# The reciprocal of the softmax denominators moves from the middle to the end of VectorE's step

## The chip, the cores and the metric

The kernel runs on one core of a Trainium2 chip. The metric is the device time of one execution in microseconds (us); a kernel's time is the median of several runs. The engines are called PE (TensorE; PEld is its weight load), DVE (VectorE), ACT (ScalarE), POOL (GpSimd) and SP (SyncE).

## The reference

128 sequences of 64 tokens with 128 features pass through one layer: cross-attention with 16 heads of 8 features, and a feed-forward network of which each token uses one of 8 experts. Cut to what matters:

```python
def xattn(Q, K, V, Wq, bq, Wk, bk, Wv, bv, Wo, bo):     # 16 heads of 8
    q = split_heads(Q @ Wq.T + bq); k = split_heads(K @ Wk.T + bk); v = split_heads(V @ Wv.T + bv)
    scores = einsum('bhqd,bhkd->bhqk', q, k) / sqrt(8)
    probs = softmax(scores, axis=-1)
    out = einsum('bhqk,bhkd->bhqd', probs, v)
    return merge_heads(out) @ Wo.T + bo

def ffn(x, Wr, br, W1, b1, W2, b2):                      # 8 experts, 128 -> 512 -> 128
    expert = argmax(x @ Wr.T + br)
    y_e = relu(x @ W1[e].T + b1[e]) @ W2[e].T + b2[e]
    return y_e of each token's own expert

x = x + xattn(layernorm(x), ctx, ctx, ...)
x = x + ffn(layernorm(x), ...)
```

## The kernel before

The 8192 tokens are 64 tiles of 128 (two sequences a tile). The program is written by hand, engine by engine: each engine has its own list of instructions, runs it in order, and waits on semaphores that the others raise. There are four stretches: projections (to some 70 us), attention (to some 340 us), the end of the routing, and the expert network (from some 380 us).

In the attention stretch every engine goes through the same loop of steps, and step n of each engine works on several tiles at once, at different stages of their way. On PE, step n holds in this order: the scores of tile n (L809); the first half of the transposes of tile n-2's exponentials (L796); the product that spreads the reciprocals over the heads' features (L833, tile n-8); the output projection (L837, tile n-9); small work for the routing (L844, L851, L853, L862); the second half of the transposes (L796); numerators (L879) and denominators (L888) of tile n-3. On DVE, step n holds: the maximum over each head's scores of tile n (L627) and their subtraction (L635); `OT`, the numerators times the spread reciprocals, of tile n-8 (L651); the addition of the projected output to `X` for tile n-9 (L654); bn_stats of tile n-10 (L664), and at some steps the moments (L525 to L533, where n mod 8 is 1), the seed of an inverse root (L674 to L680, where n mod 8 is 2) or routing work for a batch of eight tiles. The scores of tile n and n+1 lie in different PSUM banks, so that PE can be one tile ahead of DVE.

The denominators of four tiles are a group: they are added up in one half of PSUM bank 5, and one reciprocal turns the whole group into `RD` (128x128). Group g is tiles 4g to 4g+3. DVE takes its reciprocal in step 4g+7. PE's step 4g+7 holds, as its last part, the denominators of tile 4g+4, the first of group g+1. They go to the other half of the same bank, and PE waits ahead of them for the reciprocals of all groups up to g:

```python
g, t = divmod(m, GT)              # m = n - 3, GT = 4
if t == 0:
    need(pe, rd_done, g)          # L884
at = P * (g % 2)
for z in range(2):
    for c in range(4):
        last = nc.tensor.matmul(bank(5)[32 * c:32 * c + 32, at:at + P], ones[:, t, z, :], ...)
last.then_inc(od_done, 1)
```

PE's next instruction is the first of the scores of step n+1. PE also waits for a group's reciprocal ahead of the first L833 of that group, in step 4g+8. DVE waits ahead of the reciprocal for the denominators of tile 4g+3, which are the end of PE's step 4g+6. POOL spreads the values of each tile into `VP` (L410) after the denominators of an earlier tile, and at the end of a batch sends eight tiles' rows to HBM (L425).

Of the kernel before, what the change touches and what calls it, by code (L numbers as in the profile page):

```python
# [14 lines left out]
P = 128  # L15
# [5 lines left out]
GT = 4  # L21
NG = NT // GT
# [58 lines left out]
L_RD = 7  # L81
# [40 lines left out]
def need(eng, sem, value):  # L122

    if not isinstance(value, int) or value > 0:
        eng.wait_ge(sem, value)
# [25 lines left out]
def build(nc, x, ctxT, wts, we, w2, con, pad, ids, out):  # L151
# [6 lines left out]
    with ctx:  # L158
        def sb(name, *shape, dt=f32):
            return ctx.enter_context(nc.sbuf_tensor(name, list(shape), dt))  # L160

        def sem(name):
            return ctx.enter_context(nc.semaphore(name))
# [47 lines left out]
        RD = sb("RD", P, 2, P)  # L211
# [36 lines left out]
        def bank(k, n=1):  # L248
            return PS[:, 512 * k:512 * (k + n)]
# [13 lines left out]
        pt_done, pt_ready, od_done, rd_done, ot_ready = (sem(n) for n in ("pt_done", "pt_ready", "od_done", "rd_done", "ot_ready"))  # L263
# [255 lines left out]
        def _(dve):  # L519
            def moments(n, st, ms, mean, var, half, gap, mv, var_read):  # L520


                m0, m1, v0, v1 = (st[:, :, k] for k in (1, 4, 2, 5))
                need(dve, mv, n)
                nc.vector.tensor_tensor(ms[:, 0, :], m0, m1, ALU.add)  # L525
                nc.vector.tensor_tensor(ms[:, 1, :], v0, v1, ALU.add)
                nc.vector.tensor_tensor(ms[:, 2, :], m0, m1, ALU.subtract).then_inc(half, 1)
                dve.wait_ge(half, n + 1)
                need(dve, *var_read)
                nc.vector.tensor_scalar(mean, ms[:, 0, :], 0.5, None, ALU.mult)  # L530
                nc.vector.scalar_tensor_tensor(ms[:, 3, :], ms[:, 2, :], 0.25, ms[:, 2, :], ALU.mult, ALU.mult).then_inc(gap, 1)
                dve.wait_ge(gap, n + 1)
                nc.vector.scalar_tensor_tensor(var, ms[:, 1, :], 1.0 / D, ms[:, 3, :], ALU.mult, ALU.add).then_inc(mv, 1)  # L533
# [87 lines left out]
            def stage2(s):  # L621
                n = s.n
                stage3_early(s)
                sc = bank(2 * (n % 2), 2).rearrange("p (h k) -> p h k", h=H)
                if n < NT:
                    dve.wait_ge(s_done, n + 1)
                    nc.vector.tensor_reduce(MX[:, n % 2, :], sc, axis=AX.X, op=ALU.max).then_inc(mx_done, 1)  # L627
                g, late = divmod(n - L_RD, GT)
                if late == 0 and 0 <= g < NG:
                    dve.wait_ge(od_done, GT * g + GT)  # L630
                    nc.vector.reciprocal(RD[:, g % 2, :], bank(5)[:, P * (g % 2):P * (g % 2) + P]).then_inc(rd_done, 1)
                if n < NT:
                    dve.wait_ge(mx_done, n + 1)
                    need(dve, pt_done, 2 * (n - 2))
                    nc.vector.tensor_tensor(SB[:, n % 3].rearrange("p (h k) -> p h k", h=H), sc,  # L635
                                            MX[:, n % 2, :].unsqueeze(2).to_broadcast([P, H, SEQ]), ALU.subtract).then_inc(sub_done, 1)


                need(dve, rdx_done, min(n - L_MUL + 1, NT))
                need(dve, wo_done, min(n - L_X1 + 1, NT))  # L640
                for i in range(4):
                    j = s.batch(M_LG + 2 * i)
                    if j is not None:
                        dve.wait_ge(lgp_done, 4 * j + i + 1)
                j = s.batch(M_RANK)
                if j is not None:
                    dve.wait_ge(rank_done, j + 1)
                m = n - L_MUL
                if 0 <= m < NT:
                    dve.wait_ge(num_kept, m + 1)  # L650
                    nc.vector.tensor_tensor(OT[:, m % 2, :], bank(7)[:, 0:P], NUM[:, m % 8, :], ALU.mult).then_inc(ot_ready, 1)  # L651
                m = n - L_X1
                if 0 <= m < NT:
                    nc.vector.tensor_tensor(X[:, m, 0:D], bank(7)[:, P:2 * P], X[:, m, 0:D], ALU.add).then_inc(x1_done, 1)  # L654
                stage3_late(s)

            def stage3_late(s):
                for t in range(ST):
                    j = s.batch(M_BN + t)
                    if j is not None:  # L660
                        if isinstance(s.n, int):
                            dve.wait_ge(x1_done, j * ST + t + 1)
                        x1 = X[:, bass.ds(j * ST + t, 1), 0:D].rearrange("p a d -> p (a d)")
                        nc.vector.bn_stats(STAT2[:, t, :], x1).then_inc(stat2, 1)  # L664
                j = s.batch(M_MOM)
                if j is not None:
                    dve.wait_ge(stat2, ST * j + ST)
                    moments(j, STAT2, MS2, X[:, bass.ds(j * ST, ST), MU], VAR2[:], half2, gap2, mv2, (inv_step, INV_STEPS * j))
                j = s.batch(M_SEED)
                if j is not None:  # L670


                    dve.wait_ge(mv2, j + 1)
                    nc.vector.tensor_scalar(VAR2[:], VAR2[:], EPS, None, ALU.add).then_inc(seed_step, 1)  # L674
                    dve.wait_ge(seed_step, 4 * j + 1)
                    nc.vector.tensor_scalar(YY[:].bitcast(i32), VAR2[:].bitcast(i32), 1, None, ALU.logical_shift_right).then_inc(seed_step, 1)
                    dve.wait_ge(seed_step, 4 * j + 2)
                    nc.vector.tensor_scalar(Y[:].bitcast(i32), YY[:].bitcast(i32), -1.0, float(0x5f3759df), ALU.mult, ALU.add).then_inc(seed_step, 1)
                    dve.wait_ge(seed_step, 4 * j + 3)
                    nc.vector.tensor_scalar(HALF[:], VAR2[:], 0.5, None, ALU.mult).then_inc(seed_step, 1)  # L680
                    dve.wait_ge(seed_step, 4 * j + 4)

            dve.wait_ge(xb_done, NG)
            each_step(stage2)


# [285 lines left out]
```

## Time and profile before

| | us |
|---|---|
| median of 3 runs | 535.09 |
| lowest, highest | 534.26, 535.75 |
| the profiled execution | 536.78 |
| its span in the trace | 534.9 |
| PE busy in the span | 465.3 (87%) |
| DVE busy | 408.5 (76%) |
| ACT busy | 311.0 (58%) |
| POOL busy | 235.2 (44%) |

The profile is one execution; its time is its span with 1.9 us around it. Busy time of an engine is the time in which one of its instructions runs; a share over the whole span mixes stretches with different limits, so the attention stretch has to be looked at by itself. The granted clock of PE is 1.00 where it runs at 2.4 GHz and 0.50 at 1.2 GHz.

### The profile page before, as it was taken

The page shows a single profiled execution, that of the slowest core. Times are in us where ns is not written, and L with a number is a line of the kernel's source. Part 1 is how long each engine was busy: PE and PEld are TensorE (multiplying, and loading weights), DVE is VectorE, ACT ScalarE, POOL GpSimd, SP SyncE. Part 2 cuts the span into 40 slices and gives each one's busy share as a digit, 9 for nine tenths or more (in the row PEclk, how much of TensorE's full clock was granted, in tenths as well). Part 3 has the DMA queues.
Part 4 walks back from the last instruction along what each step waited for, and adds up shares of the span by engine and source line. Part 5 has one row for each costly group of instructions (what it writes and reads, how often), then busy time and mean ns, then how long its engine had stood idle before and what let it go on. Part 6 is the DMA issues. An engine that isn't in the chain of part 4 may idle for free.

```text
span 534.9 us, 19185 instructions
## 1 busy us (share of the span) xinstructions
PE 465.3 (87%) x6467; PEld 352.4 (66%) x6468; DVE 408.5 (76%) x1053; ACT 311.0 (58%) x584; POOL 235.2 (44%) x391
## 2 busy tenths in 40 slices
PE   1999968899999999999999999430499999999991
PEld 1666624566666666666666667320399999999991
DVE  5799755787998999999899895426287777777871
ACT  1577755566666666666666665000377777777770
POOL 7233311212226637365472745474245554455452
PEclk9999989999999999999999999655599999999996
DMA  8355211000011112021110106611222222222210
GB/s 260 102 151 148 70 25 18 17 18 19 19 21 40 37 23 55 17 48 35 29 49 18 48 13 219 219 40 46 73 57 74 58 67 64 68 68 65 67 56 0
DMA packets 32480, 33.74 MB, mean 63 GB/s; under 512 B 6419, under 2 KB 25750, under 8 KB 32160
## 3 DMA queue, kind: packets, MB, share of 16 engines
q1 hardware_dynamic: 28096, 24.33, 17.3%
q0 software_dynamic: 4320, 8.53, 4.8%
q8 instruction: 43, 0.70, 0.6%
q14 instruction: 21, 0.17, 0.1%
HBM read 19.10 MB, written 9.99 MB: 54 GB/s over the span
## 4 chain that ended last, share of the span: by engine, by line
PE 71%; issue 10%; DVE 10%; POOL 4%; DMA 2%; ACT 1%; SPq 1%; DVEq 0%; POOLq 0%
PE PS L918 13%; PE PS L931 12%; PE PS L809 10%; PE PS L796 10%; PE PS L879 5%; PE PS L888 4%; PE PS L780 3%; PE PS L785 3%; DVE MX L627 3%; POOL rows L425 3%; PE PS L767 3%; PE PS L833 2%; PE PS L837 2%; PE PS L904 2%; PE PS L844 1%
## 5 line engine op out<-in xcount | busy, mean ns | idle before, releaser
L410 POOL TENSOR_TENSOR VP<-BIG,C 128x128 f32<-128x128 f32 x128 | 56.2, 460 | 130.8 <-PE PS L888 127.0
L435 POOL DMA_INDIRECT out<-SB,BIG x71 | 68.9, 971 | 80.4 <-DVE SB L751 77.2
L627 DVE TENSOR_REDUCE MX<-PS 128x16 f32<-128x1024 f32 x64 | 78.2, 1222 | 29.9 <-PE PS L809 28.4
L796 PEld LDWEIGHTS PS<-C,SB 128*128 128x128 f32 x512 | 54.3, 142 | 67.5 <-ACT SB L494 34.9
L796 PE MATMUL PS<-C,SB 128*128 128x128 f32 x512 | 85.0, 289 | 6.9 <-ACT PT L482 6.6
L510 ACT COPY KM<-BIG 128x644 f32 x71 | 51.7, 729 | 55.4 <-PE PS L918 28.2
L918 PE MATMUL PS<-BIG,KM 128*128 128x128 f32 x568 | 79.7, 283 | 0.4
L494 ACT ACTIVATE SB<-SB 128x1024 f32<-128x1024 f32 x64 | 67.7, 1058 | 21.2 <-DVE SB L635 19.5
L635 DVE TENSOR_TENSOR SB<-PS,MX 128x1024 f32<-128x1024 f32 x64 | 77.4, 1209 | 1.7
L931 PE MATMUL PS<-KM,SB 128*128 x568 | 75.2, 276 | 0.6 <-ACT SB L514 0.6
L918 PEld LDWEIGHTS PS<-BIG,KM 128*128 128x128 f32 x568 | 71.8, 196 | 2.9 <-issue 1.7
L425 POOL DMA_INDIRECT rows<-X,DESTI x64 | 63.8, 996 | 22.3 <-issue 15.7
L809 PE MATMUL PS<-KM,BIG 64*64 64x512 f32 x512 | 70.6, 622 | 2.6 <-DVE SB L635 1.8
L931 PEld LDWEIGHTS PS<-KM,SB 128*128 128x128 f32 x568 | 69.1, 192 | 0.8 <-issue 0.8
L482 ACT COPY PT<-PS 128x512 f32<-128x512 f32 x64 | 37.4, 585 | 37.4 <-PE PS L796 34.9
L491 ACT COPY PT<-PS 128x512 f32<-128x512 f32 x64 | 37.5, 586 | 36.7 <-PE PS L796 36.7
L740 DVE TENSOR_TENSOR SB<-PS,KM 128x512 f32<-128x512 f32 x71 | 49.0, 691 | 11.0 <-PE PS L918 7.1
L514 ACT ACTIVATE SB<-SB 128x512 f32<-128x512 f32 x71 | 44.6, 628 | 6.6 <-DVE SB L740 6.6
L879 PE MATMUL PS<-PT,VP 128*32 128x64 f32 x2048 | 41.9, 222 | 0.0
L888 PE MATMUL PS<-PT,C 128*32 128x128 f32 x1024 | 39.9, 273 | 0.5
L879 PEld LDWEIGHTS PS<-PT,VP 128*32 128x32 f32 x2048 | 31.6, 110 | 10.6 <-issue 10.5
L369 POOL TENSOR_TENSOR X<-X,W 128x512 f32 x16 | 17.4, 1090 | 40.5 <-DVE SB L543 37.3
(108 smaller groups left out, 697.2 us busy)
## 6 DMA issues: line engine op xcount, KB each, us to landing
BIG<-rows SPq DMA_DIRECT2D x71, 66.0 KB
X<-in_x SPq DMA_DIRECT2D x16, 256.0 KB, 3.2
PT<-in_ctxT SPq DMA_DIRECT2D x16, 256.0 KB, 2.8
KM<-BIG SPq DMA_DIRECT2D x256, 16.0 KB
BIG<-in_we SPq DMA_DIRECT2D x1, 2576.0 KB, 11.4
KM<-in_w SPq DMA_DIRECT2D x1, 2048.0 KB
out<-SB,BIG POOLq DMA_INDIRECT x71
rows<-X,DESTI POOLq DMA_INDIRECT x64
```

Source lines behind the costliest of these rows:

```text
L410: last = nc.gpsimd.tensor_tensor(dst, v, own, ALU.mult)
L425: nc.gpsimd.indirect_dma_start(out=rows, out_offset=bass.IndirectOffsetOnAxis(ap=DESTI[:, t:t + 1], axis=0), in_=X[:, j * ST + t, :], in_o ...
L435: nc.gpsimd.indirect_dma_start(out=out, out_offset=bass.IndirectOffsetOnAxis(ap=RT[:, s.r, ID:ID + 1].bitcast(i32), axis=0), in_=YO[:, s.r ...
L494: nc.scalar.activation(SB[:, n % 3, :], SB[:, n % 3, :], ACT.Exp, scale=SCALE).then_inc(exp_done, 1)
L627: nc.vector.tensor_reduce(MX[:, n % 2, :], sc, axis=AX.X, op=ALU.max).then_inc(mx_done, 1)
L635: nc.vector.tensor_tensor(SB[:, n % 3].rearrange("p (h k) -> p h k", h=H), sc, MX[:, n % 2, :].unsqueeze(2).to_broadcast([P, H, SEQ]), ALU ...
L796: last = nc.tensor.transpose(bank(4)[:, i * P:(i + 1) * P], SB[:, n % 3, hp * P:(hp + 1) * P], ident)
L809: last = nc.tensor.matmul(bank(2 * (n % 2) + g)[SEQ * b:SEQ * (b + 1), :], QT[rows_g, n * P + SEQ * b:n * P + SEQ * (b + 1)], KM[rows_g, g ...
L879: nc.tensor.matmul(bank(6)[32 * c:32 * c + 32, at:at + SEQ], VP[:, m % 2, b, 2 * c + z, :], PT[:, m % 2, 2 * c + z, SEQ * b:SEQ * b + SEQ] ...
L888: last = nc.tensor.matmul(bank(5)[32 * c:32 * c + 32, at:at + P], ones[:, t, z, :], PT[:, m % 2, 2 * c + z, :], start=t == 0 and z == 0, s ...
L918: last = nc.tensor.matmul(bank(2 + b.r % 2)[:, c * P:(c + 1) * P], WS[:, b.r % 4, c * P:(c + 1) * P], XT[:, b.r % 2, :], start=True, stop= ...
L931: last = nc.tensor.matmul(bank(4 + b.r % 2)[:, 0:D], HT[:, b.r % 2, c * P:(c + 1) * P], w, start=c == 0, stop=c == FC - 1)
```

## The change

The wait for the group's denominators and the reciprocal are taken from between the maximum and the subtraction, and stand at the end of DVE's step, behind `OT`, `X`, bn_stats and what else the step holds:

```diff
                 if n < NT:
                     dve.wait_ge(s_done, n + 1)
                     nc.vector.tensor_reduce(MX[:, n % 2, :], sc, axis=AX.X, op=ALU.max).then_inc(mx_done, 1)
-                g, late = divmod(n - L_RD, GT)
-                if late == 0 and 0 <= g < NG:
-                    dve.wait_ge(od_done, GT * g + GT)
-                    nc.vector.reciprocal(RD[:, g % 2, :], bank(5)[:, P * (g % 2):P * (g % 2) + P]).then_inc(rd_done, 1)
                 if n < NT:
                     dve.wait_ge(mx_done, n + 1)
                     need(dve, pt_done, 2 * (n - 2))
...
                 if 0 <= m < NT:
                     nc.vector.tensor_tensor(X[:, m, 0:D], bank(7)[:, P:2 * P], X[:, m, 0:D], ALU.add).then_inc(x1_done, 1)
                 stage3_late(s)
+                g, late = divmod(n - L_RD, GT)
+                if late == 0 and 0 <= g < NG:
+                    dve.wait_ge(od_done, GT * g + GT)
+                    nc.vector.reciprocal(RD[:, g % 2, :], bank(5)[:, P * (g % 2):P * (g % 2) + P]).then_inc(rd_done, 1)
```

On DVE, one whole step with a reciprocal (step 15, of group 2) and the start of the next before the change; a row names line, operation, what is written from what, and the semaphores waited for:

```order
187 L627 TENSOR_REDUCE MX<-PS 128x16 [waits s_done]
188 L631 RECIPROCAL RD<-PS 128x128 [waits od_done]
189 L635 TENSOR_TENSOR SB<-PS,MX 128x1024 [waits pt_done,mx_done]
190 L651 TENSOR_TENSOR OT<-PS,NUM 128x128 [waits num_kept,wo_done,rdx_done]
191 L654 TENSOR_TENSOR X<-PS,X 128x128
192 L664 BN_STATS STAT<-X 128x6 [waits x1_done]
193 L627 TENSOR_REDUCE MX<-PS 128x16 [waits s_done]
```

The same step of DVE in the changed kernel, where the subtraction is L631, OT L647, X L650 and the reciprocal L655:

```order
187 L627 TENSOR_REDUCE MX<-PS 128x16 [waits s_done]
188 L631 TENSOR_TENSOR SB<-PS,MX 128x1024 [waits pt_done,mx_done]
189 L647 TENSOR_TENSOR OT<-PS,NUM 128x128 [waits num_kept,wo_done,rdx_done]
190 L650 TENSOR_TENSOR X<-PS,X 128x128
191 L664 BN_STATS STAT<-X 128x6 [waits x1_done]
192 L655 RECIPROCAL RD<-PS 128x128 [waits od_done]
193 L627 TENSOR_REDUCE MX<-PS 128x16 [waits s_done]
```

The reciprocal has moved past four instructions. On PE, whose list is the same in both kernels, the end of step 7 and the start of step 8, around the denominators that open group 1:

```order
110 L879 MATMUL PS<-PT,VP 32x64 [waits num_kept,vp_done,pt_ready]
111 L879 MATMUL PS<-PT,VP 32x64 x15
112 L888 MATMUL PS<-PT,C 32x128 [waits rd_done]
113 L888 MATMUL PS<-PT,C 32x128 x7
114 L809 MATMUL PS<-KM,BIG 64x512 [waits sub_done,km_in0]
115 L809 MATMUL PS<-KM,BIG 64x512 x3
```

Nothing moved here: the wait for the reciprocal (rd_done) stands ahead of the denominators, and the scores of the next tile behind them.

## Rows read from the trace of the kernel before

**Rows 1.** The page: busy time, and the granted clock in 40 slices.

```profile
PE 465.3 (87%) x6467; PEld 352.4 (66%) x6468; DVE 408.5 (76%) x1053; ACT 311.0 (58%) x584; POOL 235.2 (44%) x391
...
PEclk9999989999999999999999999655599999999996
```

**Rows 2.** Windows: us and instructions by engine, granted clock, DMA share, GB/s.

```profile
120.00:200.00 80.00, 79.74 (x1446) 53.51 (x1438) 73.09 (x148) 51.06 (x91) 31.77 (x75) 1.00 0.12 26
```

**Rows 3.** Waits of PE from 85 to 325 us: us in total, times, longest.

```profile
PE PS L796 <- ACT PT L482: 3.6, 7, 0.7
```

**Rows 4.** Timeline, step 39: start, us, engine, line, operation, count.

```profile
224.81 1.09 PE L809 MATMUL PS<-KM,BIG 64*64 64x512 f32 x8
...
225.96 1.22 DVE L627 TENSOR_REDUCE MX<-PS 128x16 f32<-128x1024 f32 x1
...
227.10 0.95 DVE L631 RECIPROCAL RD<-PS 128x128 f32<-128x128 f32 x1
...
227.97 1.16 DVE L635 TENSOR_TENSOR SB<-PS,MX 128x1024 f32<-128x1024 f32 x1
228.21 0.62 PE L888 MATMUL PS<-PT,C 128*32 128x128 f32 x16
228.76 1.09 PE L809 MATMUL PS<-KM,BIG 64*64 64x512 f32 x8
```

**Rows 5.** Timeline, step 35: scores, maximum, reciprocal, and the denominators' weight load.

```profile
208.49 1.09 PE L809 MATMUL PS<-KM,BIG 64*64 64x512 f32 x8
...
210.03 1.22 DVE L627 TENSOR_REDUCE MX<-PS 128x16 f32<-128x1024 f32 x1
...
211.17 0.94 DVE L631 RECIPROCAL RD<-PS 128x128 f32<-128x128 f32 x1
...
212.16 0.38 PEld L888 LDWEIGHTS PS<-PT,C 128*32 128x32 f32 x16 [0.24 <-DVE RD L631]
```

**Rows 6.** Instructions that touch RD: ns min/median/max; who waited for the reciprocal.

```profile
L631 DVE RECIPROCAL RD<-PS x16: 945/947/957, 99.0 to 335.1; 128x128 f32<-128x128 f32 x16
...
  PEld PS L888: 1.4, 6
```

**Rows 7.** Timeline, DVE in step 38, which has no reciprocal.

```profile
221.81 1.22 DVE L627 TENSOR_REDUCE MX<-PS 128x16 f32<-128x1024 f32 x1
...
223.07 1.22 DVE L635 TENSOR_TENSOR SB<-PS,MX 128x1024 f32<-128x1024 f32 x1
...
224.21 0.28 DVE L651 TENSOR_TENSOR OT<-PS,NUM 128x128 f32<-128x128 f32 x1
...
224.41 0.28 DVE L654 TENSOR_TENSOR X<-PS,X 128x128 f32<-128x128 f32 x1
224.61 0.28 DVE L664 BATCH_NORM_STATS2 STAT<-X 128x6 f32<-128x128 f32 x1
```

**Rows 8.** Timeline, DVE at the end of the attention stretch.

```profile
335.15 0.96 DVE L631 RECIPROCAL RD<-PS 128x128 f32<-128x128 f32 x1
...
341.81 0.22 DVE L586 TENSOR_TENSOR PREF<-PS,X 128x64 f32<-128x64 f32 x1 [3.36 <-POOL X L390]
```

**Rows 9.** Timeline of PE with its waits in brackets, and windows of half a microsecond.

```profile
74.53 1.09 PE L809 MATMUL PS<-KM,BIG 64*64 64x512 f32 x8 [1.81 <-DVE SB L635]
...
78.48 1.12 PE L796 MATMUL PS<-C,SB 128*128 128x128 f32 x4 [1.98 <-ACT PT L482]
79.52 1.98 PE L809 MATMUL PS<-KM,BIG 64*64 64x512 f32 x8
...
336.50 0.49 PE L833 MATMUL PS<-RD,C 128*128 128x128 f32 x2 [1.29 <-DVE X L654]
...
75.50:76.00 0.50, 0.50 (x7) 0.39 (x4) 0.47 (x2) 0.07 (x1) 0.00 (x0) 0.91 0.09 16
...
82.50:83.00 0.50, 0.06 (x1) 0.00 (x0) 0.47 (x2) 0.41 (x1) 0.00 (x0) 0.76 0.00 0
...
337.50:338.00 0.50, 0.06 (x1) 0.00 (x0) 0.24 (x2) 0.00 (x0) 0.50 (x1) 1.00 0.71 264
```

## The prediction

> **What bounds the kernel now.** I read the page's busy shares first, then a table of windows over the attention stage, then the order of instructions in single steps. The page has PE busy in 87% of the span, with a granted clock of nine tenths or more over nearly the whole attention stage [rows 1]. One window of 80 us inside that stage is sharper: PE busy 79.74 of 80.00 us at a granted clock of 1.00, which is 2.4 GHz, DVE 73.09 [rows 2]. So PE never pauses there and DVE is close behind it. Every microsecond by which PE is made to wait in this stage is added to the stage, since PE has no idle time in which to catch up. A list of PE's own waits over 85 to 325 us holds nothing but 3.6 us for ACT's copies [rows 3].
>
> The step is the unit. Step 39 is one with a reciprocal: PE starts its scores at 224.81, DVE's maximum starts at 225.96 (1.15 later, when the scores are there), the reciprocal at 227.10, the subtraction at 227.97; PE starts the denominators at 228.21 and the next step's scores at 228.76 [rows 4]. The step has taken 3.95 us, like its neighbours. The reciprocal ended at 227.10 + 0.95 = 228.05, and the denominators started 0.16 after that. They are the place that matters: in a step in which the reciprocal of group g stands, PE's denominators open group g+1, and they wait for rd_done of group g. Scores of the next tile, and everything else on PE, are queued behind them. So the reciprocal has had 0.16 us to spare in such a step, no more.
>
> In six steps it has none. Step 35 follows two steps in which DVE also works on the moments and the seed of a batch of eight tiles, so that its maximum starts 210.03 - 208.49 = 1.54 us after the scores' start instead of 1.15, and PE's denominators wait 0.24 us for the reciprocal, until 212.16 [rows 5]. The waits for the reciprocal are 1.4 us in all, 6 times; there are 16 reciprocals of 0.947 us [rows 6].
>
> **The change, part by part.** No instruction is added or taken away, and PE's, ACT's, POOL's and SP's queues stay as they are. On DVE sixteen reciprocals move past the subtraction, the multiplication (OT), the addition (X) and the bn_stats of their step. No DMA is issued by any of these.
>
> What it gives: the subtraction comes 0.87 us earlier in these steps (227.97 - 227.10) and with it the exponential and, two steps on, the first transposes. I cost this gain at nothing. PE does not wait for the exponential anywhere between 85 and 325 us; the only wait before its transposes is for ACT's copies [rows 3].
>
> What it costs: where the reciprocal now ends. From a step without one: subtraction 1.26 after the maximum's start (223.07 - 221.81), OT 1.14 after the subtraction's start (224.21 - 223.07), X 0.20 later, bn_stats 0.20 later [rows 7]. The next instruction I take to start another 0.20 later, as that spacing has it. Counted from the start of PE's scores: 1.15 + 1.26 + 1.14 + 0.20 + 0.20 + 0.20 = 4.15 for the reciprocal's start, + 0.95 for its run, + 0.04 from its end to PE's release (211.17 + 0.95 to 212.16 [rows 5]) = 5.14. The denominators stand at 228.21 - 224.81 = 3.40 now. So PE waits 1.74 us at that place, and its scores, and so DVE's next maximum, come 1.74 us later. DVE stands idle for the same time, since its own next maximum needs those scores: the stall goes round the two engines and nothing else fills it.
>
> Fifteen of the sixteen reciprocals release denominators (groups 1 to 15 open in steps 7, 11, ... 63).
> - Steps 11, 15, 23, 31, 39, 47, 55, 63: 8 x 1.74 = 13.9 us.
> - Steps 19, 27, 35, 43, 51, 59, behind moments and seed: the maximum is 0.39 later, so the denominators would start at 5.53 where they start at 212.16 - 208.49 = 3.67 now: 1.86 each, 6 x 1.86 = 11.2 us.
> - Step 7 has no OT, X or bn_stats yet: 5.14 - 0.60 - 3.40 = 1.1 us.
> - Step 67, the last reciprocal, has no scores and no denominators behind it. It moves by some 0.6 us, from 335.15. The next thing the end depends on there is DVE's L586, which waits 3.36 us for POOL until 341.81 [rows 8]. That wait covers it; without the cover it would be 0.6 us.
>
> The sum is 26.2 us. The bounds of its one guessed spacing (bn_stats to reciprocal, 0.1 to 0.3) move it by 15 x 0.1 = 1.5 us either way. The profiled execution took 536.78 us (span 534.9 and 1.9 around it), so it would take 563.0; the median of the runs shown, 535.09, lies 1.7 below it, so on that scale it is **561.3**.
>
> **The clock** is the cost that the trace of before bounds only loosely. PE has no lone wait of 1.7 us in the middle of dense work now. The nearest row is at the start of the stage: PE waited 1.81 us until 74.53, was at work again, and then its granted clock dropped (0.91 over 75.5 to 76.0, so at about 75.95) to one half, 1.2 GHz, and was back only at about 82.75 (0.76 over 82.5 to 83.0) [rows 9]. A shorter wait, 1.29 us before 336.50, was followed by full clock at 337.5 to 338.0 still [rows 9]. The waits to come (1.74, and 1.86 + 0.27 = 2.13 in six steps) lie at the size of the one behind which it fell. What a fall costs: eight score matmuls took 1.98 us at half clock [rows 9] and 1.09 at full [rows 4], 1.8 times as long, so each microsecond at half clock loses 0.45. The stretch of before lasted 6.8 us: 3.1 us at most. But PE could not fill that stretch, it waited 1.98 us in it for ACT [rows 9]; in the middle of the stage it is not held up so. I take half of it, 1.5 us a fall, between nothing and 3.1.
>
> By the Trainium skill (TensorE: Matmul & The Clock Gate, section "HAM oscillation — how this bites in real kernels") a wait before each burst of matmuls can let the clock drop each time, so that every burst starts cold. By that rule all fifteen waits would pay, and the time would be that of the third case below; the fall behind the 1.81 us wait agrees with it, the full clock behind the 1.29 us one does not, and no run here shows a lone wait in dense work.
>
> **The cases.**
> - *Clock holds.* The stall alone: 561.3 us (559.8 to 562.8). For it: the clock held through the 1.29 us wait and has never moved between 83 and 338 us. Against it: the fall behind 1.81 us. Chance 0.28.
> - *Clock falls behind about half of the waits.* Eight falls x 1.5 = 12.0: **573.3 us**. With 4 falls at 1.5 to 11 at 2 it is 567 to 583. For it: the waits' size lies at the edge, and one that is at an edge will sometimes decide one way and sometimes the other. Chance 0.42; the likeliest.
> - *It falls behind nearly every wait.* 15 x 1.5 = 22.5: 583.8 us; at 3.1 each 607.8. Chance 0.25.
> - *Not slower.* The wait would have to be covered: if PE reached the denominators 1.74 us later than now in these steps, the moved reciprocal would be ready in time, and the earlier subtraction would be all that is left. That needs something else that holds PE up by over 1.74 us between scores and denominators; ACT's copies are the only candidate in the list, at 3.6 us for 240 us of the stage, seven waits of at most 0.7 [rows 3]. If it were so the time would be 535, at best 535.1 - 3.6 = 531.5. Chance 0.03.
> - *The change doesn't do what it says* (the denominators do not wait for the reciprocal of the group before, but for one further back). Then nothing changes: 535. The six waits that have the reciprocal as their releaser speak against it [rows 6]. Chance 0.02.
>
> The prediction is 573 us. The range of 8 in 10 runs from the lower end of the first case, 560, to 592, which holds the first two cases and about half of the third. Within 0.3% (1.6 us) a measurement of this kernel can't be told from no change; the last two cases share 0.05 there: faster 0.02, same 0.02, slower 0.96.
>
> **What would show it.** In the profile after: PE's weight load of the denominators waits for the reciprocal 15 times, 8 x 1.74 + 6 x 2.13 + 1.1 = 27.8 us in all, where it was 1.4. The reciprocal starts 0.2 us behind the bn_stats. The step with a reciprocal lasts 5.7 us (3.95 + 1.74) and the others 3.96 as now, unless the granted clock in 85 to 350 us is under 1.00, which decides between the first three cases: at 1.00 throughout it is the first. DVE's maximum behind a reciprocal waits about 1.7 us for PE. The FFN from the first row load on lasts as long as before. The prediction is wrong if PE reaches the denominators late for another reason, or if a fall of the clock costs several times the 1.5 us.

## The result and the profile after

The changed kernel takes 571.99 us (571.66 to 573.21, 4 runs) against 535.3 us (534.26 to 535.75): a ratio of 1.067, 95% interval 1.064 to 1.070. The profiled execution took 572.01 us with a span of 569.9, 35.1 more than the span before. Lines of the changed kernel are named as it numbers them: subtraction L631, OT L647, X L650, reciprocal L655; lines from L656 on are those of before.

From the page of the changed kernel, busy shares and granted clock, to be set beside [rows 1]:

```profile
PE 475.8 (83%) x6467; PEld 357.7 (63%) x6468; DVE 411.8 (72%) x1053; ACT 312.6 (55%) x584; POOL 235.4 (41%) x391
...
PEclk9999989999999799898998999955569999999997
```

Next, windows from the scores of step 4 to the scores of step 63, first of the changed kernel, then of the one before (columns as in [rows 2]):

```profile
83.78:354.08 270.30, 242.95 (x4208) 158.93 (x4204) 214.36 (x416) 150.90 (x263) 107.15 (x235) 0.96 0.11 26
```

```profile
84.84:321.46 236.62, 232.25 (x4208) 154.13 (x4204) 211.90 (x416) 149.74 (x263) 106.80 (x235) 1.00 0.13 29
```

The same instructions take 270.30 us instead of 236.62, 33.68 more. PE's idle time in it rises from 236.62 - 232.25 = 4.4 to 27.4 us, and the granted clock falls from 1.00 to 0.96. What is left of the 35.1 lies around it: 1.06 less ahead of it, the stall of step 63 behind it, and 0.66 more in the expert network, which lasts 153.9 us from its first transpose (416.02) to the end of the span, and 153.2 (from 381.63) before. Its granted clock comes back 6.4 us behind that transpose (at about 422.4), and 4.9 behind it before (at about 386.5).

What PE waited for between 85 and 360 us in the changed kernel, in us, times and the longest, where [rows 3] had the second line alone:

```profile
PE PS L888 <- DVE RD L655: 25.0, 15, 2.0
PE PS L796 <- ACT PT L482: 3.6, 7, 0.7
```

And who waited for the reciprocal, where [rows 6] had 1.4 us, 6 times:

```profile
  PEld PS L888: 27.4, 15
  PE PS L888: 25.0, 15
```

One wait is new on PE's list, 15 times, at the place of the denominators. Step 39, the one of [rows 4], in the changed kernel:

```profile
242.12 1.09 PE L809 MATMUL PS<-KM,BIG 64*64 64x512 f32 x8
...
243.27 1.22 DVE L627 TENSOR_REDUCE MX<-PS 128x16 f32<-128x1024 f32 x1
...
246.07 0.28 DVE L664 BATCH_NORM_STATS2 STAT<-X 128x6 f32<-128x128 f32 x1
246.27 0.94 DVE L655 RECIPROCAL RD<-PS 128x128 f32<-128x128 f32 x1
247.26 0.65 PE L888 MATMUL PS<-PT,C 128*32 128x128 f32 x16 [1.55 <-DVE RD L655]
247.83 1.09 PE L809 MATMUL PS<-KM,BIG 64*64 64x512 f32 x8
...
248.99 1.23 DVE L627 TENSOR_REDUCE MX<-PS 128x16 f32<-128x1024 f32 x1 [1.79 <-PE PS L809]
```

The denominators start 247.26 - 242.12 = 5.14 us after the scores, where they stood at 3.40 [rows 4]. The step takes 5.71 us instead of 3.95. DVE then waits 1.79 us for the next scores: the stall has gone round, as nothing else was there to do.

Step 35, the one of [rows 5], shows the second part of the loss. Here are PE and its weight load, and below them the granted clock in windows of half a microsecond:

```profile
227.98 0.63 PEld L888 LDWEIGHTS PS<-PT,C 128*32 128x32 f32 x16 [2.09 <-DVE RD L655]
...
228.99 1.98 PE L809 MATMUL PS<-KM,BIG 64*64 64x512 f32 x8
...
230.91 0.81 PE L796 MATMUL PS<-C,SB 128*128 128x128 f32 x4
```

```profile
227.00:227.50 0.50, 0.00 (x0) 0.00 (x0) 0.50 (x2) 0.50 (x1) 0.34 (x3) 1.00 0.08 12
227.50:228.00 0.50, 0.02 (x4) 0.02 (x4) 0.42 (x1) 0.06 (x1) 0.09 (x1) 0.87 0.10 21
228.00:228.50 0.50, 0.50 (x12) 0.47 (x16) 0.00 (x0) 0.00 (x0) 0.00 (x0) 0.50 0.18 33
...
231.00:231.50 0.50, 0.50 (x4) 0.50 (x5) 0.46 (x1) 0.00 (x0) 0.34 (x3) 0.72 0.16 29
231.50:232.00 0.50, 0.50 (x7) 0.50 (x5) 0.50 (x1) 0.24 (x1) 0.17 (x1) 1.00 0.02 4
```

The wait is 2.09 us, and near its end, at about 227.9, the clock drops to 1.2 GHz; it is back at about 231.3. The scores behind it take 1.98 us where those of step 39 take 1.09.

### The profile page after: what moved, and what is told of

It reads as the page before. It is cut to its first block, busy times and chain, and to the rows that moved or that the text cites. A ratio compares the mean times of both kernels' runs of the same rounds, so it can differ in the third digit from the quotient of the medians.

```text
span 569.9 us, 19185 instructions
## 1 busy us (share of the span) xinstructions
PE 475.8 (83%) x6467; PEld 357.7 (63%) x6468; DVE 411.8 (72%) x1053; ACT 312.6 (55%) x584; POOL 235.4 (41%) x391
## 4 chain that ended last, share of the span: by engine, by line
PE 65%; DVE 15%; issue 10%; POOL 4%; DMA 2%; ACT 1%; SPq 1%; DVEq 0%; POOLq 0%
PE PS L918 12%; PE PS L931 11%; PE PS L809 10%; PE PS L796 8%; DVE MX L627 6%; PE PS L888 4%; PE PS L879 4%; PE PS L780 3%; PE PS L785 3%; POOL rows L425 3%; PE PS L767 3%; DVE RD L655 2%; PE PS L904 1%; PE PS L833 1%; PE PS L844 1%
## 5 line engine op out<-in xcount | busy, mean ns | idle before, releaser
L796 PEld LDWEIGHTS PS<-C,SB 128*128 128x128 f32 x512 | 56.1, 146 | 70.8 <-ACT SB L494 34.1
L796 PE MATMUL PS<-C,SB 128*128 128x128 f32 x512 | 86.8, 294 | 6.8 <-ACT PT L482 6.5
L631 DVE TENSOR_TENSOR SB<-PS,MX 128x1024 f32<-128x1024 f32 x64 | 78.4, 1224 | 2.2
L809 PE MATMUL PS<-KM,BIG 64*64 64x512 f32 x512 | 74.6, 656 | 2.6 <-DVE SB L631 1.8
L888 PE MATMUL PS<-PT,C 128*32 128x128 f32 x1024 | 41.4, 280 | 25.0 <-DVE RD L655 25.0
L491 ACT COPY PT<-PS 128x512 f32<-128x512 f32 x64 | 37.5, 586 | 38.1 <-PE PS L796 37.3
L888 PEld LDWEIGHTS PS<-PT,C 128*32 128x32 f32 x1024 | 26.1, 112 | 27.5 <-DVE RD L655 27.4
```

Source lines behind the costliest of these rows:

```text
L796: last = nc.tensor.transpose(bank(4)[:, i * P:(i + 1) * P], SB[:, n % 3, hp * P:(hp + 1) * P], ident)
L809: last = nc.tensor.matmul(bank(2 * (n % 2) + g)[SEQ * b:SEQ * (b + 1), :], QT[rows_g, n * P + SEQ * b:n * P + SEQ * (b + 1)], KM[rows_g, g ...
```

## The experiments

In all of them the kernel before was run on the same chip; its medians there were 536.58, 536.63 and 536.65 us for the three groups of runs, 1.3 us above that of the first comparison. A measured difference below is against the group's own. "Falls" are drops of the granted clock to one half between 85 us and the end of the attention stage, counted in the profile's windows.

**1. The reciprocal right behind the subtraction.** It moves past one instruction instead of four:

```diff
                                             MX[:, n % 2, :].unsqueeze(2).to_broadcast([P, H, SEQ]), ALU.subtract).then_inc(sub_done, 1)
+                g, late = divmod(n - L_RD, GT)
+                if late == 0 and 0 <= g < NG:
+                    dve.wait_ge(od_done, GT * g + GT)
+                    nc.vector.reciprocal(RD[:, g % 2, :], ...)
                 need(dve, rdx_done, min(n - L_MUL + 1, NT))
```

> The reciprocal stands right behind the subtraction, ahead of OT, X and bn_stats. Theory (PE's denominators wait for the reciprocal, and each us of that wait is lost): the reciprocal ends 0.60 us earlier than at the step's end, so the waits are 1.14 us in nine steps and 1.53 in the six steps behind moments and seed (0.27 of which was there before), 9 x 1.14 + 6 x 1.26 = 17.8 us more than the kernel before, 553.1 us, with the granted clock at 1.00 from 85 us on. Rival (what costs is that the reciprocal is no longer between maximum and subtraction at all, whatever its place behind): the same as the changed kernel, about 572 us.

Measured: 555.34 us, 18.8 over its before (ratio 1.035, 1.031 to 1.038). No falls. Who waited for the reciprocal (here the denominators are L889):

```profile
  PEld PS L889: 19.8, 15
  PE PS L889: 17.4, 15
```

The loss goes with where the reciprocal ends. The waits were 1.12 or 1.13 in nine steps as expected; three of the six others were 1.71 or 1.72 instead of 1.53, 0.5 of the 1.0 us by which the sum was low.

**2 and 3. Half of the reciprocals at the end.** The two places both hold the block, with `g % 2` as a further condition; kernel 2 moves those of steps 7, 15, ... 63, kernel 3 those of steps 11, 19, ... 59 and 67:

```diff
-                if late == 0 and 0 <= g < NG:
+                if late == 0 and 0 <= g < NG and g % 2 == 1:    # between maximum and subtraction; kernel 3: == 0
...
+                if late == 0 and 0 <= g < NG and g % 2 == 0:    # at the step's end; kernel 3: == 1
```

> Only the reciprocals of steps 7, 15, ... 63 (eight of sixteen) stand at the step's end, the others between maximum and subtraction as before. Theory: 1.14 + 7 x 1.74 = 13.3 us more than before, 548.6 us; by the trace of the changed kernel no fall of the clock follows these waits of 1.72 us. Rival (the clock falls behind any wait of this size once it comes at the right moment): some falls at 1.5 us each, 551 to 556 us.

> The complement: only the reciprocals of steps 11, 19, ... 59 and 67 stand at the step's end. Theory: stalls of 1.74 + 6 x 1.86 = 12.9 us, and falls of the clock behind the waits of 2.1 us, five or six at 1.5 to 3 us: 535.3 + 12.9 + 8 to 11 = 556 to 559 us. Rival (the clock falls for another reason, such as the sum of all fifteen waits): no falls, 548.2 us.

Measured: 548.88 us (+12.3; ratio 1.023, 1.020 to 1.027) and 549.43 us (+12.9; 1.025, 1.020 to 1.029). Neither profile has a fall; over 85 to 338 us the granted clock is 1.00 in both. The first loss is 1.0 us under the 13.3 worked out for its stalls, the second is the 12.9 worked out, and the two add up to 25.2 where the sum for all sixteen is 26.2. For the clock, my expectation for kernel 3 was wrong: its waits are at least as long (2.09 to 2.30 us) as the five behind which the changed kernel's clock fell, and in the profiled execution it held through all six. So length alone does not decide. (Another execution of kernel 3 took 551.75 us at a mean clock of 0.939, where the other three had 0.945 or 0.946; it may have had a fall, which no trace shows.)

**4. The reciprocal ahead of bn_stats.** The block stands between X and `stage3_late(s)`, so that the waits are one bn_stats shorter.

> The reciprocal stands behind X and ahead of bn_stats. The waits become 0.2 us shorter, 1.52 us and 1.90 us, in all steps but step 7. Theory of the stall: 26.2 - 14 x 0.2 = 23.4 us more than before. If the clock still falls behind waits of 1.90 us: 535.3 + 23.4 + 9 = 567.7 us. If a wait of 1.90 us is short enough for the clock to hold: 558.7 us, at a granted clock of 1.00 from 85 us on.

Measured: 565.43 us (+28.9; 1.052, 1.049 to 1.057). Its four executions were 569.45, 563.17, 566.28 and 564.58 us, with mean granted clocks over the span of 0.930, 0.941, 0.935 and 0.936: the same program, and another share of the time at half clock each time. The kernel before, which has no such waits, varies too, by less: 534.4 to 537.7 us and 0.941 to 0.947 in this group. That the difference lies in the falls behind the waits is likely, but not shown, as the profile is of the first execution alone. It has waits of 1.52 us in the eight steps with OT and no lateness, no fall behind any, and waits of 1.89 to 2.11 in the six others, with a fall behind five. A wait of 1.9 us is enough then, but not each time. The median is 2.3 us under the 567.7 that I had for falls; the profiled execution, with five of them, is the slowest of the four.

**5. All long waits.** The changed kernel with two idle bn_stats ahead of the reciprocal in seven steps:

```diff
                 stage3_late(s)
+                g, late = divmod(n - L_RD, GT)
+                if late == 0 and g % 2 == 0 and 2 <= g < NG:
+                    for k in range(2):
+                        nc.vector.bn_stats(SCR[:, g, k, :], X[:, n - M_BN, 0:D])
```

> The changed kernel with two more bn_stats (into a scratch tile, for nothing) ahead of the reciprocal in steps 15, 23, ... 63. Their waits become 1.72 + 0.40 = 2.12 us, as long as those of the six steps behind moments and seed. The stalls alone give 26.2 + 7 x 0.4 = 29.0 us, 564.3 us. Theory A (a wait of about 2 us lets the clock fall when it comes at certain moments, whichever step it is in): falls in some of thirteen steps, those of steps 23, 31, ... among them, some 8 at 1.5 us: 573 to 581 us. Theory B (the clock falls only behind the steps that follow moments and seed): five falls as in the changed kernel, about 572 us, none behind steps 15, 23, ... 63.

Measured: 582.97 us (+46.3; 1.087, 1.083 to 1.091), 2.0 us above the range for theory A; the kernel before is 1.3 us slower in this group. The reciprocal is waited for 15 times, 30.1 us in all. The profile has 10 falls behind thirteen waits of 2.1 us, where I had some 8, four of them behind steps 15, 31, 47 and 63, which in the changed kernel had waits of 1.72 us and no fall. So it is the wait, and not what the steps of moments and seed do (theory B), that lets the clock fall.

**6. Dense work in place of the short waits.** Kernel 3, with a matmul repeated in steps 15, 23, ... 63:

```diff
-                    nc.tensor.matmul(bank(7)[:, 0:P], C[:, C_SEL + P * t:C_SEL + P * (t + 1)], RD[:, g % 2, :],
-                                     start=True, stop=True).then_inc(rdx_done, 1)
+                    for k in range(9 if 15 <= n < NT and n % 8 == 7 else 1):
+                        last = nc.tensor.matmul(bank(7)[:, 0:P], C[:, C_SEL + P * t:C_SEL + P * (t + 1)], RD[:, g % 2, :],
+                                                start=True, stop=True)
+                    last.then_inc(rdx_done, 1)
```

> The kernel in which only the reciprocals of steps 11, 19, ... 59 and 67 stand at the end (no fall of the clock in its profile), with L833 done nine times over in steps 15, 23, ... 63: 8 x 0.22 = 1.76 us more of dense PE work in the steps in which the changed kernel has its wait of 1.72 us. So the long waits come at the same distances as in the changed kernel, with dense work where that has its shorter waits. Stalls 12.9 us and 7 x 1.76 = 12.3 us of work: 560.5 us without falls. Theory A (what decides besides the wait's length is when it comes): falls behind the 2.1 us waits as in the changed kernel, 566 to 570 us. Theory C (it takes the shorter waits in between as well): no falls, 560.5 us.

Measured: 573.93 us (568.95 to 574.59; +37.3; 1.067, 1.062 to 1.072), with six falls behind the six long waits. Theory C, that it takes the short waits in between as well, falls: there are none between the long ones here. Step 35 in kernel 3 and in this one, PE alone (the denominators are L892 and L894, the scores L813 in both):

```profile
219.04 0.64 PE L892 MATMUL PS<-PT,C 128*32 128x128 f32 x16 [1.94 <-DVE RD L659]
219.62 1.09 PE L813 MATMUL PS<-KM,BIG 64*64 64x512 f32 x8
```

```profile
229.46 0.91 PE L894 MATMUL PS<-PT,C 128*32 128x128 f32 x16 [1.93 <-DVE RD L659]
230.30 1.99 PE L813 MATMUL PS<-KM,BIG 64*64 64x512 f32 x8
```

The same wait, to 0.01 us, and full clock behind it in one, half in the other. So something beside the wait's length decides. That it is the moment at which the wait comes, as theory A has it, fits, but is not shown by itself. The time was 4 to 8 us above what I had for theory A. Of that, 1.3 are the kernel before's own in this group, and 1.5 the first of the six falls, which cost twice the others (steps 20 and 21 are 2.68 + 0.41 us over 3.96). Another 1.6 lie in the expert network, which no edit touched: 154.8 us from its first transpose (417.72) to the end of the span, 153.2 before.

**7. The reciprocal at the end, but the denominators don't wait for it.** ACT copies the group's denominators out of PSUM at the start of its step, the reciprocal reads the copy, and PE waits for the copy. A plain later wait (PE writing one half of bank 5 while DVE reads the other) wasn't tried: PE and DVE would use one PSUM bank at the same time with nothing to order them, and no run here shows what that does.

```diff
                     nc.scalar.copy(NUM[:, (n - 4) % 8, :], ...).then_inc(num_kept, 1)
+                    g, late = divmod(n - L_RD, GT)
+                    if late == 0 and 0 <= g < NG:
+                        need(act, rd_done, g - 1)
+                        nc.scalar.copy(DN[:, g % 2, :], bank(5)[:, P * (g % 2):P * (g % 2) + P]).then_inc(dn_done, 1)
...
-                    dve.wait_ge(od_done, GT * g + GT)
-                    nc.vector.reciprocal(RD[:, g % 2, :], bank(5)[:, P * (g % 2):P * (g % 2) + P]).then_inc(rd_done, 1)
+                    dve.wait_ge(dn_done, g + 1)
+                    nc.vector.reciprocal(RD[:, g % 2, :], DN[:, g % 2, :]).then_inc(rd_done, 1)
...
-                        need(pe, rd_done, g)
+                        need(pe, dn_done, g)
```

> The reciprocal stays at the step's end, but ACT first copies the group's denominators from PSUM to SBUF at the start of its step, and PE's denominators wait for that copy (0.27 us, done some 1 us after the scores) and no longer for the reciprocal. Theory (the whole loss is PE's wait at the denominators and the clock behind it): the loss goes, and so do the six waits of 0.27 us of the kernel before: 535.3 - 1.6 = 533.7 us; the spread of the reciprocals (L833 in the next step, 5.37 us after the scores) is just met by a reciprocal that ends at 5.10, or 0.1 us late in six steps, so 533.7 to 534.5. Rival (DVE's step itself is the bound, or the later reciprocal is waited for at L833): 540 us or more.

Measured: 536.73 us (12 runs) against 536.63, ratio 1.000, 0.998 to 1.002. With the reciprocal as late as in the changed kernel, the whole loss is gone. PE's waits between 85 and 325 us (L802 are the transposes, L839 is the spread of the reciprocals), one row of its weight load's, and its windows:

```profile
PE PS L802 <- ACT PT L488: 3.6, 7, 0.7
PE PS L839 <- DVE RD L661: 0.3, 2, 0.2
```

```profile
PEld PS L839 <- issue: 1.5, 6, 0.4
```

```profile
83.84:320.47 236.63, 232.37 (x4208) 154.08 (x4204) 213.40 (x416) 152.35 (x277) 107.23 (x235) 1.00 0.13 30
```

The gain that I expected beyond that, 1.6 us from the six waits of the kernel before, did not come: 236.63 us for the stretch that took 236.62. The steps behind moments and seed are 3.96 us long now, but the ones after them (20, 28, ...) 4.12 to 4.32. There PE's weight load of the spread sits idle, six times, 1.5 us in all. The profile names no releaser, but each time it starts 0.12 us after the reciprocal's end (0.27 or more in the other steps of that stretch): the value itself comes late. So the wait of before has moved to the reciprocal's next user; the 0.1 us that I allowed for it was 0.2 in four steps and 0.4 in two.

**8. The reciprocal ahead of the maximum**, the block moved up by one `if`.

> The reciprocal stands ahead of the maximum in the same step. Its denominators are there since the end of PE's step before, and DVE waits for the scores at that place in most steps. Theory: it ends about 1.1 us earlier than in the kernel before, so that PE's denominators wait nowhere for it; the six waits of 0.27 us go: 533.7 us. The maximum comes up to 0.95 us later in these steps and the subtraction about where it is now. Rival (the later maximum holds up ACT's exponential or PE's next scores): 536 us or more.

Measured: 535.78 us (12 runs) against 536.63, ratio 0.999, 0.997 to 1.002: no difference that can be told, so the gain to 533.7 that I expected is not there. PE does not wait for the reciprocal anywhere, but again the 0.3 us come back in steps 20, 28, ... (4.26 to 4.46 us): PE waits for ACT's copies ahead of its transposes 12 times between 85 and 325 us, 4.2 us in all, where it was 7 times and 3.6. From the scores of step 4 to those of step 63 it is 237.27 us, 236.62 before.

**9. Longer waits at kernel 3's places.** Four idle bn_stats, as in 5, ahead of the reciprocal in steps 19, 27, ... 59.

> The kernel in which only the reciprocals of steps 11, 19, ... 59 and 67 stand at the end, with four more bn_stats (into a scratch tile, for nothing) ahead of the reciprocal in steps 19, 27, ... 59. Their waits become 2.09 + 0.80 = 2.9 us; they come 35 us apart, and in this kernel's own form without the extra work none of the six was followed by a fall in the profile. Stalls 12.9 + 6 x 0.8 = 17.7 us: some 554 us without falls. Theory A (the longer a wait, the more of the moments at which it comes let the clock fall): five or six falls of 1.5 to 3 us, 563 to 570 us. Theory D (only the distance from wait to wait decides, not the length): few falls or none, 554 to 557 us.

Measured: 563.09 us (559.28 to 565.59; +26.4; 1.048, 1.041 to 1.055). The six waits are 2.86 or 2.87 us long, and four of them (steps 27, 35, 51 and 59) are followed by a fall, where I had five or six. That is four more than with 2.1 us at the same places, as theory A has it; the distance from wait to wait is 35 us instead of 34 as well, so length and moment are not cleanly apart here.

## Why the prediction was right

**What bounds the kernel, and the place of the loss.** Right. PE's denominators wait for the reciprocal 15 times, 27.4 us in all, where 27.8 were forecast, and with that wait taken from the reciprocal (experiment 7) the same order on DVE costs nothing.

**The stall's size.** Right to 0.02 us a step: denominators at 5.14 to 5.15 and, in the six late steps, 5.52 to 5.55 us after the scores, for 5.14 and 5.53; steps of 5.72 us; step 7's wait 1.13 for 1.14. The sum of 26.2 us stands; experiments 2 and 3 find it in its two halves, to 1.0 us. One reading beside it is off: step 39 is not like all its neighbours, as step 38 takes 4.15 us. Every eighth step (22, 30, ... 62) does, in both kernels, so it drops out of the difference.

**The gain costed at nothing.** Right: the subtraction comes earlier, and on PE's list the waits for ACT's copies are the 3.6 us, 7 times, of before.

**Step 67.** Right: the next thing there is still DVE's L586, which waits 3.38 us for POOL, 3.36 before. PE's last spread does wait 1.85 us there, now for the reciprocal (1.29 for DVE's `X` before), but L586 starts 22.10 us after the scores of step 63, 20.35 before: 1.75 more, no more than the stall of step 63 itself.

**The expert network.** It was to last as long as before, and takes 0.66 us more; its clock came back later, as said above.

**The clock.** The likeliest case came: the clock fell behind some of the waits and not behind others. Its count was too high: 5 falls, where the prediction had 8. That 8 was about half of fifteen, not worked out from rows, and the case took waits of 1.74 and 2.13 us alike; in the trace the falls came behind five of the six waits of 2.09 to 2.12 us and none of the eight of 1.72. By the steps' lengths, the first cost 6.72 + 4.29 - 2 x 3.96 = 3.1 us and the other four 1.5 to 1.6 each, 9.3 us in all against 12.0. So the term of the sum that was mis-sized is the number of falls; with 24.4 us of stalls up to the scores of step 63 the 9.3 us make 33.7, the 33.68 by which that stretch grew.

The price of 1.5 us was half of an upper bound, and fits four of the five, which left the clock at 1.2 GHz for 3.4 us each. The reason given for the half, that PE could not fill the stretch of before, does not hold for the first: it lasted 6.8 us (190.3 to 197.15), as long as that stretch, and cost the full 3.1, though PE had no wait in it (columns as in [rows 2]):

```profile
190.50:191.00 0.50, 0.50 (x4) 0.00 (x0) 0.00 (x0) 0.00 (x0) 0.47 (x2) 0.50 0.09 16
...
193.00:193.50 0.50, 0.50 (x5) 0.50 (x4) 0.50 (x1) 0.00 (x0) 0.00 (x0) 0.50 0.02 4
...
196.50:197.00 0.50, 0.50 (x4) 0.22 (x8) 0.00 (x0) 0.27 (x1) 0.34 (x1) 0.50 0.18 33
```

The case in which the clock holds is refuted by the windows, and so is the third, by which every wait would have paid. The prediction took this third case for what follows from the Trainium skill (TensorE: Matmul & The Clock Gate, section "HAM oscillation — how this bites in real kernels"). The kernel in that section of the Trainium skill waits some 3 to 5 us for DMA ahead of each burst of matmuls and starts each burst cold. Those waits are longer than all fifteen here, so the prediction read more into the section than it says; here five waits of some 2.1 us were followed by a fall and ten of 1.13 to 2.09 us were not.

**The time.** 573 was forecast, 571.99 measured. On the scale of the profiled execution, 563.0 + 9.3 = 572.3 against 572.01. On the forecast's own scale the falls that came make 561.3 + 9.3 = 570.6. So the forecast came so near in part by luck: 2.7 us too many for falls, and 1.4 us that it didn't have, about what separates executions of the kernel before (534.26 to 535.75 us, and 536.78 for the profiled one).

What stays open is what beside a wait's length decides whether the clock falls. The same program gave other shares of half clock in other executions (experiment 4), which suggests that it isn't in the program alone.

## What to carry to other kernels

Before moving an instruction on an engine that has time, look for who waits for its result, and subtract: here it had 0.16 us to spare and its end was moved by 1.9. Where the busiest engine waits, the wait is lost in full, and in these runs one of some two microseconds could cost 1.5 to 3.1 us more at half clock. Where the wait is for a buffer and not for the value, a cheap copy on a third engine takes it away, and the slow instruction then only has to be in time for whoever needs the value (in experiment 7 it was late for it by 1.5 us in all).

## What the runs showed of the hardware

The granted clock fell in the middle of dense work behind single waits of PE. Over all profiles of the changed kernel and experiments 1 to 6 and 9, it fell behind none of the 46 waits of 1.12 to 1.72 us at the denominators, and behind 30 of the 43 of 1.89 to 2.87 us: 5 of 6 in the changed kernel, none of 6, 5 of 6, 10 of 13, 6 of 6 and 4 of 6 in experiments 3, 4, 5, 6 and 9. The drop does not come at one point: it lies between 0.15 us ahead of the wait's end (experiment 5, step 15) and 1.5 us behind it (experiment 5, step 31). Of the 30, 23 left PE at 1.2 GHz for 3.4 us and cost about 1.5 us each where the steps show it (PE's scores took 1.98 us instead of 1.09 while they lasted); seven left it there for 6.8 us and cost about 3.
